# An attention layer on one core: half of the softmax denominators' additions move from GpSimd to accumulating DMAs, and the order of the work around them changes

## What is computed

```python
xn = ln(layernorm(x))                              # (b, n, 128)
q  = lin(xn, Wq, bq).reshape(b, n, 16, 8) / sqrt(8)
k  = lin(xn, Wk, bk).reshape(b, n, 16, 8)
score = softmax(einsum('bihd,bjhd->bhij', q, k))   # over j, 64 pairs of batch and head, 1024 x 1024 each
v  = lin(xn, Wv, bv).reshape(b, n, 8, 8)           # 8 value heads, shared by the 16 query heads
out  = einsum('bhij,bjrd->bihrd', score, v)        # every head reads all 64 value columns
comp = softmax(concat([qv, out]) @ Ws.T + bs, axis=3)   # weights over the 8 value heads
out  = (comp * out).sum(axis=3)
# then a projection, a residual, a layer norm and two feed-forward blocks, one with ternary weights
```

## Time and profile before

| | |
|---|---|
| median of 3 executions | 1245.37 us (1241.57 to 2449.64) |
| the profiled execution | 1243.4 us, span 1241.6 us |
| busy PE, DVE, ACT, POOL | 1184.0, 960.4, 757.6, 956.4 us |
| 97.8 to 1070.0 us (groups' steady part): PE busy | 970.06 of 972.20 us |
| mean share of the DMA engines in that stretch | 0.46 |

### The profile page before, as it was taken

One profiled execution on the slowest core, in us unless ns is written; L12 is line 12 of the kernel. 1 busy time (PEld: TensorE's weight loads), 2 busy tenths in 40 slices (PEclk: granted clock), 3 DMA queues, 4 the chain that ended last, 5 costly groups with the idle time before them and its releaser, 6 DMA issues. The chain is left out here.

```text
span 1241.6 us, 27803 instructions
## 1 busy us (share of the span) xinstructions
PE 1184.0 (95%) x7997; PEld 538.2 (43%) x7997; DVE 960.4 (77%) x2145; ACT 757.6 (61%) x1463; POOL 956.4 (77%) x561
## 2 busy tenths in 40 slices
PE   5599999999999999999999999999999999977898
PEld 3134444444444444444444444444444444425675
DVE  6676778788888887878788787788878888697752
ACT  3056666666666666667666666666666666644443
POOL 4257898989898988888888889897978888873321
PEclk9589999999999999999999999999999999988999
DMA  4424545454444344444445354544444434330000
GB/s 115 120 65 92 113 95 117 104 116 96 104 102 104 90 113 104 104 106 99 115 99 113 83 116 98 117 105 105 104 104 103 104 88 103 70 68 1 18 25 26
DMA packets 60372, 115.52 MB, mean 93 GB/s; under 512 B 6656, under 2 KB 25568, under 8 KB 60336
## 3 DMA queue, kind: packets, MB, share of 16 engines
q0 software_dynamic: 18784, 67.70, 28.8%
q1 hardware_dynamic: 40770, 47.04, 11.8%
q10 hardware_dynamic: 782, 0.33, 0.1%
HBM read 22.51 MB, written 8.39 MB: 25 GB/s over the span
## 5 line engine op out<-in xcount | busy, mean ns | idle before, releaser
L1234 DVE TENSOR_REDUCE rowmax<-row_bank 128x1 f32<-128x512 f32 x1024 | 662.6, 685 | 191.0 <-PE row_bank L989 182.4
L1181 ACT ACTIVATE prob<-col_bank 128x512 f32<-128x512 f32 x1024 | 555.0, 594 | 273.3 <-PE col_bank L1008 272.1
L1018 PE MATMUL out_bank<-prob,v_op 128*64 128x512 f32 x2048 | 533.3, 594 | 0.4 <-issue 0.2
L1343 POOL TENSOR_TENSOR addend<-prob 128x1024 f32<-128x1024 f32 x128 | 316.4, 2472 | 48.3 <-ACT prob L1181 48.1
L1343 POOL TENSOR_TENSOR quad<-prob 128x1024 f32<-128x1024 f32 x128 | 329.0, 2570 | 28.0 <-ACT prob L1181 27.7
L989 PE MATMUL row_bank<-k_op,q_op 72*64 72x512 bf16 x2048 | 325.7, 388 | 14.6 <-DMA q_op<-q_parts 9.7
L1008 PE MATMUL col_bank<-q_op,k_op 74*64 74x512 bf16 x2048 | 319.5, 383 | 2.2 <-ACT prob L1181 1.2
L1008 PEld LDWEIGHTS col_bank<-q_op,k_op 74*64 74x64 bf16 x2048 | 117.5, 109 | 242.6 <-ACT prob L1181 148.1
L989 PEld LDWEIGHTS row_bank<-k_op,q_op 72*64 72x64 bf16 x2048 | 120.2, 109 | 150.0 <-DVE rowmax L1234 46.3
L1018 PEld LDWEIGHTS out_bank<-prob,v_op 128*64 128x64 f32 x2048 | 151.5, 136 | 71.9 <-issue 11.2
L1348 POOL DMA_DIRECT2D quad<-addend x128 | 112.4, 878 | 77.5 <-POOL addend L1343 73.0
(11 more groups left out here) (197 smaller groups left out, 822.5 us busy)
## 6 DMA issues: line engine op xcount, KB each, us to landing
quad<-addend POOLq DMA_DIRECT2D x128, 512.0 KB, 5.5
v_op<-v_all SPq DMA_DIRECT2D x64, 256.0 KB, 6.5
k_op<-k_parts SPq DMA_DIRECT2D x64, 144.0 KB
q_op<-q_parts SPq DMA_DIRECT2D x192, 48.0 KB
q_parts<-along_parts SPq DMA_DIRECT2D x11, 192.0 KB, 2.1
k_parts<-along_parts SPq DMA_DIRECT2D x33, 64.0 KB, 2.1
out<-y_out SPq DMA_DIRECT2D x8, 256.0 KB, 2.3
q_op<-max_rows SPq DMA_DIRECT2D x64, 4.0 KB
```

Source lines behind the costliest of these rows:

```text
L1018: last = nc.tensor.matmul(out_bank[ih * VW:(ih + 1) * VW, :], v_op[slot][:, t, :], halves(prob[:, t, :])[:, :, ih, :], start=(t == 0), sto ...
L1181: nc.scalar.activation(prob[:, t, h * HALF:(h + 1) * HALF], col_bank[h][:, :], ACT.Exp).then_inc(exp_done, 1)
L1234: nc.vector.tensor_reduce(rowmax[:, parity, t, h:h + 1], row_bank[h][:, :], AX.X, ALU.max).then_inc(max_done, 1)
L1343: pool.tensor_tensor(dst, prob[:, 2 * k, :], prob[:, 2 * k + 1, :], ALU.add).then_inc(pair_done, 1)
```

## The change

POOL adds only the pairs (0,1) and (2,3), straight into `quad[.., 0]` and `quad[.., 1]` (`pair`). Blocks 4 to 7 are added by four accumulating DMAs that read `prob` itself (`add_prob`: n = 0 adds blocks 4 and 5, n = 1 blocks 6 and 7; the second into a `quad` waits for the first), and a fifth, `add_quads`, adds one `quad` to the other. `denominators` then reads one sum a unit, of the unit two before, at step 2: four matmuls of 256 columns. Only the last unit adds two parts. `turn_den` has two transposes, DVE's addition goes. `turn_out` moves from step 6 to step 2, `turn_max` from step 2 to step 5, and row scores run LEAD = 12 steps ahead. Small steps of the other work are moved to other steps.

```diff
+LEAD = TB + TB // 2
-            sums = self.turn_bank[:, :].rearrange("p (e k s) -> p e s k", k=2, s=32)[:, :, 0:SLOTS, :]
-            self.nc.vector.tensor_reduce(self.den[:, :, :], sums, AX.X, ALU.add).then_inc(self.den_ready, 1)
+            sums = self.turn_bank[:, 0:HALF // 2].rearrange("p (e h s) -> p h e s", h=2, s=32)[:, :, :, 0:SLOTS]
...
+            def denominators(u, slot, parts):
                 for ih in range(2):
+                    for hc in range(2):
+                        q = 32 * (2 * ih + hc)
+                        for k in range(parts):
+                            last = nc.tensor.matmul(
+                                den_bank[q:q + 32, 0:HALF // 2], onehot[:, slot, :],
+                                halves(quad[:, slot % 2, k, :])[:, 2 * hc:2 * hc + 2, ih, :],
...
+                        if t == 2 and before:
+                            if not (first and s < 2):
+                                pe.wait_ge(sum_in, DMA * (u - 1))
+                                denominators(u - 2, (s - 2) % SLOTS, 1)
...
                             turn_out(u - 1)
+                        if t == 5 and not (last and s == SLOTS - 1):
+                            turn_max(u + 1, (s + 1) % 2)
...
# ACT, ahead of the exponentials of step t
-                                act.wait_ge(pair_done, TB // 2 * u - TB // 2 + t // 2 + 1)
+                                if t < TB // 2:
+                                    act.wait_ge(pair_done, 2 * u - 1 + t // 2)
+                                else:
+                                    act.wait_ge(quad_in[t % 2], DMA * (2 * u - 1 + (t - TB // 2) // 2))
...
# POOL
+            def add_prob(u, slot, k, n):
+                pool.wait_ge(exp_done, 2 * TB * u + 2 * (TB // 2 + 2 * n + k) + 2).then_inc(mix.stood, 1)
+                if n == 0:
+                    pool.wait_ge(pair_done, 2 * u + k + 1).then_inc(mix.stood, 1)
+                else:
+                    pool.wait_ge(quad_in[k], DMA * (2 * u + 1)).then_inc(mix.stood, 1)
+                pool.dma_start(quad[:, slot % 2, k, :], prob[:, TB // 2 + 2 * n + k, :],
+                               accum_op=ALU.add).then_inc(quad_in[k], DMA)
+            def add_quads(u, slot):
+                for k in range(2):
+                    pool.wait_ge(quad_in[k], DMA * (2 * u + 2)).then_inc(mix.stood, 1)
+                pool.dma_start(quad[:, slot % 2, 0, :], quad[:, slot % 2, 1, :], accum_op=ALU.add).then_inc(sum_in, DMA)
...
             def group(G, first, along):
                 for s in range(SLOTS):
+                    if before:
+                        for k in range(2):
+                            add_prob(u - 1, sp_, k, 1)
+                    if along and s == 0:
+                        project.rstd_of(pool, G, 0)
+                    if along and s == 3:
+                        project.rest(pool, G, 0)
+                    for k in range(2):
+                        pair(u, s, k, first and s < 2)
+                    if before:
+                        add_quads(u - 1, sp_)
+                    for k in range(2):
+                        add_prob(u, s, k, 0)
...
```

More of the change, by code:

```diff
@@ L906, in attention @@
         quad = sb("quad", [P, 2, 2, SEQ])
-        addend = sb("addend", [P, 2, SEQ])
         rowmax = sb("rowmax", [P, 2, TB, 2])
@@ L1020, in values @@
                 last.then_inc(pv_done, 1)
-            def denominators(u, slot):
-                for k in range(2):
-                    pe.wait_ge(quad_in[k], DMA * (u + 1))
+            def denominators(u, slot, parts):
                 for ih in range(2):
[L1027 to L1031, removed]
+                    for hc in range(2):
[4 more added lines that the diff above has]
+                                halves(quad[:, slot % 2, k, :])[:, 2 * hc:2 * hc + 2, ih, :],
+                                start=(slot == 0 and k == 0), stop=(slot == SLOTS - 1 and k == parts - 1))
                 last.then_inc(den_done, 1)
@@ L1053, in group @@
                     before = not (first and s == 0)
-                    ahead = not (last and s >= 2)
-                    Gv, sv, sp_ = (G if s < 2 else G + 1), (s + 2) % SLOTS, (s - 1) % SLOTS
+                    sp_ = (s - 1) % SLOTS
                     for t in range(TB):
+                        av, tv = (s * TB + t + LEAD) // TB, (t + LEAD) % TB
+                        ahead, Gv, sv = not (last and av >= SLOTS), G + av // SLOTS, av % SLOTS
                         if t == 0:
@@ L1071, in group @@
                             values(u - 1, sp_, TB - 1)
[L1072 to L1083, removed]
+                        if t == 2 and before:
+                            if not (first and s < 2):
+                                if s == 2 and not first:
+                                    pe.wait_ge(denT_ready, G)
+                                pe.wait_ge(sum_in, DMA * (u - 1))
+                                denominators(u - 2, (s - 2) % SLOTS, 1)
                             if along and s == 1:
@@ L1182, in group @@
                                                  ACT.Exp).then_inc(exp_done, 1)
-                        if t == 2 and not (last and s == SLOTS - 1):
+                        if t == 5 and not (last and s == SLOTS - 1):
                             sent = s >= 1 or not first
@@ L1191, in group @@
                             take_turned(u - 1, G if s > 0 else G - 1, (s - 1) % SLOTS)
-                        if t == 6 and s == 0 and not first:
+                        if t == 4 and s == 1 and not first:
                             take_den(G - 1)
@@ L1253, in _ @@
             PLAN = {
[L1254 to L1262, removed]
+                (1, 2): [("logit sums", 0, 5)],
+                (1, 5): [("logit sums", 5, 6)],
+                (1, 6): [("logit sums", 6, 7)],
+                (1, 7): [("logit sums", 7, 8), ("denominators",)],
+                (2, 0): [("logits over denominators",)],
+                (2, 1): [("query part",)],
+                (2, 2): [("maxima",), ("shift",)],
                 (2, 4): [("totals",)],
@@ L1315, in _ @@
             last.then_inc(onehot_set, 1)
[L1316 to L1322, removed]
+            for t in range(TB):
+                for h in range(2):
+                    row_max(0, 0, t, h)
+            for step in range(3):
+                split_max(0, 0, step)
+            for t in range(LEAD - TB):
+                for h in range(2):
+                    row_max(1, 1, t, h)
             group(0, True, False, True)
@@ L1378, in _ @@
                 group(G, False, False)
+            for k in range(2):
+                add_prob(U - 1, SLOTS - 1, k, 1)
             joined.norm.root(pool, 0)
```

159 lines of the change are left out of this document (80 added, 79 removed).

## The result

The changed kernel takes 1533.1 us (median of 4 runs, 1528.71 to 1535.9), the kernel before beside it 1243.47 us. One of the four executions of the kernel before took 2449.64 us, for no known reason; the ratio goes by the others. It is 1.234, with a 95% interval of 1.231 to 1.237: the changed kernel is slower, as forecast, but by 290 us where I had 120, and outside the range. The profiled execution took 1528.7 us, its span is 1526.9 us.

What follows compares the result with a forecast made beforehand. The chain of five accumulating DMAs and loads was taken as the bound: 60 x (18.3 - 16.25) = +123 us on 1243.4, less 4 for the prologue and small tail terms, gave 1361, with the median's 0.2% 1363 us; range 1270 to 1460.

Steps and rivals of the forecast that it cites:

- PE is the bound before; what the change takes off it.: PE's instructions take 16.25 us a unit; denominators lose 0.5 us a unit, turn_den 5 us in 16 groups.
- POOL is relieved.: POOL's pair additions and DMA issues go from 12.0 us to 9.5 us a unit.
- rival 2: POOL's order: two pair additions after A1 lands delay add_quads; period 19.9 us, 1457 us in all; chance 0.12.
- The DMA engines' work: three engines at 16.9 us.: Three DMA engines carry five transfers of 2.5 us plus 4.4 us of loads: 16.9 us a unit, 9.4 before.
- The chain: 18.3 us a period.: From add_quads' issue to B1's landing, dependent accumulating DMAs with loads between them take one period, 18.3 us a unit.
- 18.9 us with all loads inside: Upper case of the DMA period: all 4.4 us of loads fall within the 14.5 us of five transfers.
- loads in that time: Load packets take turns with accumulating ones, starting 2.2 us behind add_quads' first: 33 packets of 0.09, 3.0 us.
- chain 0.62: Dependent accumulating DMAs and loads set the period at 16.9 to 19.3 us a unit, 1278 to 1422 us; chance 0.62.
- maxima 0.08: PE waits 2 us each unit for the maxima's DMA after turn_max at step 5: 17.7 us, 1326 us; chance 0.08.
- The clock.: If PE's clock falls to 0.91, PE needs 16.6 us a unit and is still not the bound.

Runs made afterwards that it cites:

- a_13_k: The changed kernel with the maxima one step earlier and the k_op load split into three DMAs of 24 rows, same bytes: 1430.4 us, 1.151 of the kernel before.
- the light loads: The changed kernel with loads bringing one of three copies of k_op and q_op rows, and no PE wait for the maxima: 1323.7 us, ratio 1.066.
- a_nomax: The changed kernel with the maxima's DMA writing into an unread buffer from the fifth unit on and PE not waiting for it: 1532.8 us, ratio 1.233.
- a_13: The changed kernel with the maxima one step earlier, row scores 13 steps ahead, nothing left out: 1532.9 us, 1.233 of the kernel before.
- a_light: The changed kernel with loads bringing only the first of three copies of k_op and q_op rows from the second group on: 1521.0 us, ratio 1.224.

## Why the prediction was wrong

**PE is the bound before; what the change takes off it.** Right. The denominators' PE time went from 69.1 us to 42.2 us busy on the page, 0.42 us a unit for 0.5.

**POOL is relieved.** Right: 956.4 to 821.1 us busy, and rival 2 did not come: ahead of C POOL stands idle for 2.7 and 4.0 us in the timeline, its pair additions were done.

**The DMA engines' work: three engines at 16.9 us.** Right in kind: the tail of three engines in the DMA view, and a_13_k, which moved 18 packets off them and gained 1.7 us a unit. The Trainium skill's rule on the number of engines (DMA: Bandwidth & Descriptors, Why a DMA increments its semaphore by 16) is what made that edit: 24 rows without the leading broadcast. Its formula of 2.0 us and bytes over 436 GB/s (Anatomy of one DMA) would have had PE as the bound; the 2.6 us of A0 against its 1.2 us of data movement deny it again for these accumulating transfers.

**The chain: 18.3 us a period.** This step failed, in the size of its terms, not in its parts; even the upper bounds, 18.9 us with all loads inside and 19.9 by rival 2, were too low. From C's issue to the next C's, 20.96 us:

| term | predicted | measured |
|---|---|---|
| issue to first packet, last packet to next issue | 2.0 | 1.4 + 1.0 |
| five transfers | 12.5 | 13.1 (C 2.7, the others at A0's 2.6) |
| loads in that time | 3.0 of 4.4 | all, 4.4 by the rows of before |
| engines idle between queues, stores | 0.8 | what is left, 1.1 |

The largest miss is the loads, 1.4 us: the earlier trace rows shows the queues in turns while both run, and I took it that loads would start 2.2 us behind C's first packet, with 7 packets gone and at most 33 of the loads' inside. In the trace their first packet comes 8.4 us behind C's first (702.87 to 711.2), they don't start while A0 and A1 are queued ahead, and then fall wholly into B0 and B1. That all of them count agrees with the light loads: by their expectation 3.6 us less on the busiest engines, and the period fell from 20.96 to 17.50. The second miss is the transfers, 0.6 us: 2.5 us was read off the tail of a transfer, when only three engines were at work; with all 16, A0 took 2.6 and C 2.7. Start and end add 0.4 us, the rest 0.3. The first two make 2.0 us of the 2.7 us a unit, 120 us of the miss of 170.

**The rivals.** I had made them exclusive: chain 0.62, maxima 0.08. They are both there and of nearly equal length. For the time of this kernel the second adds nothing (a_nomax, a_13: 0 us), and it would have hidden a repair of the first (a_light: 12 us for 209).

**The clock.** I had it harmless at 0.91, with PE busy for 82%. It is 0.92 in the long stretch, with PE busy for 86%:
```profile
120.00:960.00 840.00, 722.86 (x4586) 299.04 (x4584) 536.31 (x1149) 440.26 (x873) 499.72 (x379) 0.92 0.76 156
```
By the table above the first loop has no place for it, but no run held the clock. In the second loop PE's time counts, and there it works at half clock for 3 us and more behind the waits.

## What to carry to other kernels

Before work is given to the DMA engines, count it for the busiest engine and not for the mean: a share of 0.46 hid three engines with 58% of their time taken (an estimate, 9.4 of 16.25 us), and a broadcast of three as the leading dimension was the reason. When one repair of a suspected bound gives nothing, look at the new trace for what waits now before dropping the theory; two loops of equal length are told apart only by taking away both. And a small DMA that PE waits for should not be issued in the same moment as large ones: moving it by one step of 1.7 us was worth 39 us where two transfers ran, 197 us where five did and the loads were light.

## What the hardware showed unexpectedly

A load of SP that is issued while two accumulating transfers are queued gets no packet for over 5 us (q1 absent from 705.55 to 710.85), for 1.6 us with none queued, though later both queues take turns. A DMA of 4 KB took 6 us from its issue to the instruction that waited for it. Behind short waits PE's granted clock fell to half where it had been at the full 2.4 GHz: in a_light PE stood 2.9 us ahead of 710.80 and worked at 0.55 in 711.70 to 714.70. In the changed kernel it stood 1.6 us ahead of 722.63, and the low clock lasted longer:
```profile
724.00:727.00 3.00, 3.00 (x14) 1.04 (x12) 1.68 (x4) 1.03 (x3) 2.23 (x3) 0.50 1.06 195
727.00:730.00 3.00, 3.00 (x16) 1.10 (x14) 1.78 (x8) 1.03 (x3) 0.00 (x0) 0.59 1.05 198
```
